# Expert weights split into bf16 pairs ahead of the expert layer instead of inside it, in a four-layer kernel on one core

## The reference

```python
logits = jnp.einsum('btd,de->bte', x, gate_w)
expert_weights, expert_indices = jax.lax.top_k(softmax(logits), 2)
for i in range(8):
    wi = jnp.where(expert_indices == i, expert_weights, 0.0).sum(-1)
    h = silu(x @ w1[i]) * (x @ w3[i])      # 256 -> 1024
    out = out + (h @ w2[i]) * wi[..., None]  # 1024 -> 256
```

## Time and profile before

| what | value |
|---|---|
| median of 3 runs | 864.96 us (863.54 to 866.54) |
| profiled execution | 865.73 us, its span in the trace 864.0 us |
| PE busy | 679.8 us, 79% of the span |
| PE weight loads | 471.9 us, 55% |
| DVE busy | 527.0 us, 61% |
| ACT busy | 410.6 us, 48% |
| POOL busy | 278.8 us, 32% |
| mean granted clock of TensorE | 0.879 of full |
| DMA | 58.41 MB, mean 68 GB/s |

### The profile page before, as it was taken

One profiled execution on the slowest core, in us unless ns is written; L12 is line 12 of the kernel. 1 busy time (PEld: TensorE's weight loads), 2 busy tenths in 40 slices (PEclk: granted clock), 3 DMA queues, 4 the chain that ended last, 5 costly groups with the idle time before them and its releaser, 6 DMA issues.

```text
span 864.0 us, 19336 instructions
## 1 busy us (share of the span) xinstructions
PE 679.8 (79%) x4571; PEld 471.9 (55%) x4615; DVE 527.0 (61%) x1371; ACT 410.6 (48%) x831; POOL 278.8 (32%) x390
## 2 busy tenths in 40 slices
PE   2999999885853991577417989898989998989992
PEld 2788887663322670466404556565656555655661
DVE  5577789985867452788785464646454555464441
ACT  1466655556874463345225444545353545553430
POOL 3111111111436001644302263535354253553421
PEclk9799999986978795555558999999999999999996
DMA  8100000000000114211270514243331525431213
GB/s 260 32 13 12 16 14 13 0 1 1 0 0 12 44 42 159 87 28 27 97 245 19 169 30 132 67 128 73 105 90 31 170 34 165 124 73 24 34 22 110
DMA packets 45844, 58.41 MB, mean 68 GB/s; under 512 B 13497, under 2 KB 39417, under 8 KB 45273
## 3 DMA queue, kind: packets, MB, share of 16 engines
q1 hardware_dynamic: 38328, 47.79, 16.9%
q0 software_dynamic: 7488, 10.31, 7.2%
HBM read 145.90 MB, written 11.80 MB: 183 GB/s over the span
## 4 chain that ended last, share of the span: by engine, by line
PE 48%; DVE 18%; issue 14%; POOL 7%; DMA 3%; ACT 3%; DVEq 2%; POOLq 1%; ACTq 1%; SPq 0%
PE psum L995 16%; PE psum L1017 7%; PE psum L718 3%; PE psum L1008 3%; POOL region L658 3%; PE psum L702 3%; PE psum L725 3%; PE psum L895 2%; PE psum L738 1%; PE psum L757 1%; PE psum L707 1%; PE psum L840 1%; PE psum L888 1%; DVE region L1358 1%; DMA region<-xrow_dram,next_token 1%
## 5 line engine op out<-in xcount | busy, mean ns | idle before, releaser
L995 PE MATMUL psum<-region 128*128 x897 | 209.6, 382 | 19.8 <-POOL pause_p L660 6.2
L995 PEld LDWEIGHTS psum<-region 128*128 128x128 bf16 x936 | 91.6, 98 | 119.1 <-issue 30.4
L1017 PE MATMUL psum<-region 128*128 x936 | 112.5, 278 | 6.2 <-DVE region L1868 3.7
L1017 PEld LDWEIGHTS psum<-region 128*128 128x128 bf16 x936 | 91.3, 100 | 22.3 <-issue 9.2
L1261 ACT ACTIVATE region<-psum 128x512 f32<-128x512 f32 x78 | 46.5, 596 | 115.0 <-PE psum L995 104.2
L1838 DVE TENSOR_TENSOR region<-psum,region 128x512 f32<-128x512 f32 x78 | 53.9, 690 | 72.9 <-ACT region L1261 62.9
L628 POOL TENSOR_TENSOR pause_p<-minus_half 128x1 f32<-128x1 f32 x37 | 7.1, 193 | 191.4 <-DVE next_token L1854 190.6
L640 POOL DMA_INDIRECT sum_dram<-region,tok_idx x39 | 62.0, 1589 | 6.6 <-issue 6.3
L1282 ACT ACTIVATE pause_a<-one_col 128x1 f32<-128x1 f32 x117 | 23.7, 202 | 84.1 <-issue 70.2
L525 POOL TENSOR_TENSOR region<-region,pair_mask 128x256 f32<-128x256 f32 x32 | 18.9, 612 | 137.8 <-ACT region L1062 137.8
L1868 DVE TENSOR_TENSOR region<-psum,region 128x1024 bf16<-128x1024 f32 x39 | 47.6, 1222 | 20.1 <-ACT region L1269 20.1
(11 more groups left out here) (304 smaller groups left out, 1386.0 us busy)
## 6 DMA issues: line engine op xcount, KB each, us to landing
region<-in_L_ffn_w SPq DMA_DIRECT2D x117, 1024.0 KB
region<-in_ctx SPq DMA_DIRECT2D x48, 128.0 KB, 2.1
region<-neg_max_dram SPq DMA_DIRECT2D x4, 1024.0 KB, 7.6
xrow_dram<-region SPq DMA_DIRECT2D x1, 2080.0 KB, 7.8
x_sb<-in_x SPq DMA_DIRECT2D x4, 512.0 KB, 7.1
sum_dram<-x_sb SPq DMA_DIRECT2D x1, 2048.0 KB, 7.5
region<-in_L_ffn_w_down SPq DMA_DIRECT2D x1, 704.0 KB, 8.1
region<-in_L_ffn_w_gate SPq DMA_DIRECT2D x1, 640.0 KB, 8.6
```

Source lines behind the costliest of these rows:

```text
L995: last = mm(psum[:, 2 * f + n, :], (xT_lo if xl else xT_hi)[:, p, k, :], weights_at(place, wl, n, k * F1 + f * FH, FH), start=(i == 0), st ...
L1017: last = mm(psum[:, 7, 0:D], (hT_lo if hl else hT_hi)[:, f, :], weights_at(place, wl, 2, f * D, D), start=(i == 0), stop=(i == 3 * (F1 // ...
```

## The change

All 24 matrices are split before the router. A matrix is a part `i` of 24: the first 18 are those of experts 2 to 7 (`EARLY_PARTS`), the last six those of experts 0 and 1.

- **Early parts, beside attention 0.** SP loads part `i` as f32 into one of three rings in the free `hT` space, POOL issues a second DMA of the same matrix that casts it to bf16 (the high part), POOL subtracts (the low part, four instructions of 512 columns), and SP stores the pair (1 MB) to `split_dram`. POOL does one part after each `mask_k`, its last four around the FFN's start. DVE and POOL wait for all 18 stores before `hT` is written.
- **Late parts, beside the front of attention 1.** SP loads them, POOL casts (four instructions) and subtracts (four), straight to where experts 0 and 1 are read from. Expert 1's pairs are also stored. SP issues these before its `gates_dram` stores, and ACT takes over the `ctx_c` loads, which SP issued before.
- **The expert layer.** SP loads the pairs of the later experts (three DMAs of 1 MB on a condition that is false for experts 0 and 1 where they are), into the slot, for tile `t` after tile `t - 3`. ACT, DVE and POOL have no weights work left, and PE waits for the loads alone. Slots hold matrix by matrix (high, low), no longer all high parts first.
- DVE's copy of two elements at the end of each batch's statistics (line 1388) is now a `tensor_reduce`. ACT asks for its Silu table ahead of the first tile. `gates_all` and `qT_c` moved within `region2`.

The diff, cut to its core:

```diff
+    EARLY_PARTS = 3 * (E - 2)
+    CHUNK = 512
...
+        early_ring = region2[:, 0:3 * 2 * PART].rearrange("p (r n) -> p r n", r=3)
...
+            def load_part(i):                                  # SP
+                view, width = weight_part(i)
+                if i >= (2 if i < EARLY_PARTS else EARLY_PARTS + 2):
+                    sp.wait_ge(part_split, i - 1)
+                sp.dma_start(whole_part(i)[0].rearrange("p (t f) -> p t f", f=width), view).then_inc(part_loaded[ring_of(i)], 16)
+
+            def store_part(i):
+                sp.wait_ge(part_split, i + 1)
+                e, n = part_of(i)
+                sp.dma_start(split_dram[e, n, :, :], whole_part(i)[1]).then_inc(part_stored[ring_of(i)], 16)
...
-            with sp.Fori(0, B // 2 - 1) as i:
-                for p in range(2):
-
-                    sp.wait_ge(t1_done, 2 * i + p + 1)
-                    sp.dma_start(ctx_sb[:, p, :], ctx_in[2 * i + (p + 2), :, :]).then_inc(ctx_loaded[p], 16)
+            load_part(0)
+            load_part(1)
+            for i in range(EARLY_PARTS + 1):
+                if i + 2 < B:
+
+                    sp.wait_ge(t1_done, i + 1)
+                    sp.dma_start(ctx_sb[:, i % 2, :], ctx_in[i + 2, :, :]).then_inc(ctx_loaded[i % 2], 16)
+                if i >= 1:
+                    store_part(i - 1)
+                    if i + 1 < EARLY_PARTS:
+                        load_part(i + 1)
...
+            load_part(EARLY_PARTS)
+            load_part(EARLY_PARTS + 1)
+            for i in range(EARLY_PARTS, PARTS):
+                if part_of(i)[0] == 1:
+                    store_part(i)
+                if i + 2 < PARTS:
+                    load_part(i + 2)
 
             sp.wait_ge(gates_read, B)
...
+            for t in range(NT + 1):
+                if t < NT:
+                    info = info_of(t)
+                    if t >= 1:
+                        sp.wait_ge(gate_up_loaded, 32 * t)
+                    if t >= 3:
+
+                        sp.wait_ge(gu_done, 2 * t - 4)
+                    load_matrix(0, info, gate_up_loaded)
+                    load_matrix(1, info, gate_up_loaded)
+                if t >= 1:
+                    if t >= 2:
+                        sp.wait_ge(down_loaded, 16 * (t - 1))
+                    if t >= 4:
+
+                        sp.wait_ge(dn_done, t - 2)
+                    load_matrix(2, info_before, down_loaded)
...
+            def cast_part(i):                                  # POOL
+                view, width = weight_part(i)
+                if i >= 3:
+                    pool.wait_ge(part_stored[ring_of(i)], 16 * (uses(i) - 1))
+                nc.gpsimd.dma_start(whole_part(i)[1][:, 0:PART].rearrange("p (t f) -> p t f", f=width), view).then_inc(part_cast[ring_of(i)], 16)
+
+            def split_part(i):
+                whole, pair = whole_part(i)
+                pool.wait_ge(part_loaded[ring_of(i)], 16 * uses(i))
+                chunks = [slice(c, c + CHUNK) for c in range(0, PART, CHUNK)]
+                if i >= EARLY_PARTS:
+                    pool.wait_ge(part_split, i)
+                    for c in chunks:
+                        nc.gpsimd.tensor_copy(pair[:, c], whole[:, c]).then_inc(part_high, 1)
+                for n, c in enumerate(chunks):
...
+                    last = nc.gpsimd.tensor_tensor(pair[:, PART:2 * PART][:, c], whole[:, c], pair[:, c], ALU.subtract)
+                last.then_inc(part_split, 1)
...
+            cast_part(0)
+            cast_part(1)
+            for b in range(1, B):
+                mask_k(b, b % 2)
+                split_part(b - 1)
+                cast_part(b + 1)
 
 
             for n, part in enumerate((slice(0, EARLY), slice(EARLY, B))):
+                if n == 1:
+                    split_part(B - 1)
+                    cast_part(B + 1)
+                    split_part(B)
                 pool.wait_ge(ln2_eps, n + 1)
                 nc.gpsimd.tensor_tensor(rstd[:, part], rstd[:, part], minus_half[:, part], ALU.pow).then_inc(rstd2_ready, 1)
+            split_part(B + 1)
+
+            for r in range(3):
+                pool.wait_ge(part_stored[r], 16 * EARLY_PARTS // 3)
...
+            for i in range(EARLY_PARTS, PARTS):
+                split_part(i)
```

204 lines of the change are left out of this document (83 added, 121 removed).

## The result

The changed kernel takes 869.2 us, the median of its 16 runs, against 866.02 us for the kernel before on the same chip: a ratio of **1.0042, 95% interval 1.0025 to 1.006**. It is slower by 0.4%, where 859 us and a gain were forecast. The profiled execution took 867.83 us (before: 865.73), with a span of 865.7 (864.0).

A forecast was written before the change was run, and what follows sets the result against it. PE was taken to bound the expert layer, with DVE near its limit at attention 0's end. The terms -27.0 + 11 + 1 + 9 = -6 and a further us made 865.7 - 7 = 859 us; own range 850 to 868, overall 842 to 890.

The forecast's parts named there:

- The DMAs: Attention 0: a load, a cast and a store fit in a batch, 9.1 of 9.9 us; +1 us for late parts.
- The collisions: End of attention 0: DVE instructions wait for whole POOL instructions at their shared port; +11 us, bounds 0 and 19.
- the rounding of `w_down`: End of attention 0: two POOL chunks meet DVE's rounding of these weights just after the masks; 2.2 us.
- the 12 scalings: End of attention 0: two POOL chunks meet DVE's scalings at 157.67 us; 2.2 us.
- the 12 norms: End of attention 0: DVE's norms at 191.42 us meet the whole split of part 16; up to 4.9, 3 us taken.
- the last norms and what is around them: End of attention 0: four norms, the maximum and line 1497's first roundings meet part 17; up to 4.9, 3.4 us taken.
- the first rival: DVE gets in between POOL's instructions and the front hides the rest; 846 us, chance 0.12.
- Attention 1: Front of attention 1: POOL's six late parts, 7.6 us each, delay the gates' store; +9 us, bounds 4 and 17.
- The experts: Expert layer: 37 tile periods of 9.25 us without weights work, 25.7 us less, and 1.3 ahead of the first tile.
- The DMA bound: Attention 0: the DMA engines become the bound and POOL waits for casted parts before masks; +30 us, 889 us, chance 0.20.
- POOL's casting DMA being long: Attention 0: POOL's DMA for `w2` parts takes 8 us and more, if time goes by rows; +18, 877 us, chance 0.09.
- The expert layer keeping its waits: Expert layer: loads come late or gathers collide with them, PE waits at each change as before; about 880 us, chance 0.04.

The follow-up runs named there:

- start_order: Changed kernel with the first two part loads ahead of the dense weights and the 35 small loads spread over the batches; ratio 0.998 to the kernel before.
- parts_early_2: Second run of the changed kernel with the first two part loads moved ahead of the 35 small loads; 869.12 us, ratio 1.0029 to the kernel before.
- chunk128: Changed kernel with POOL's casts and subtractions of the weights in chunks of 128 columns instead of 512; ratio 1.0271 to the kernel before.
- parts_early: Changed kernel with the first two part loads moved ahead of the 35 small loads, first run; ratio 1.0083 to the kernel before.

## Why the prediction was wrong

It failed by 8.7 us of span (+1.7 for -7), in the terms of its own sum:

- **The DMAs, "+1 us for parts that come a little late": the step that failed.** I asked whether the DMA engines had room, and when parts would land. I did not ask what stands behind the parts' loads in SP's queue at the start, although the change puts two loads of 1 MB right ahead of the first `ctx` loads. It cost 9.0 us: a wait of 6.5 us and the lower clock behind it. start_order gets them back. The Trainium skill (DMA: Bandwidth & Descriptors, "Queues, rings and completion order") states that on each DMA engine the descriptors of one issuing engine's queue are consumed in order; the 8.2 us of a `ctx` load behind 2 MB agree, though parts_early_2's 6.4 us with no part ahead need another reason.
- **The collisions, "+11 us", bounds 0 to 19: right in mechanism and size**, 12.8 measured. By terms: the rounding of `w_down` +1.2 for 2.2 (the mask gap over it is 12.49 us for 11.26), the 12 scalings +2.0 for 2.2 (12.97 for 10.96), the 12 norms +3.9 for 3, the last norms and what is around them +3.2 for 3.4. Of the long roundings the first grew by 0.85 us, but the mask gap over it stayed at 10.86; the second, with the small instruction behind it, cost 0.9 (1.2 forecast for both). The remaining 1.6 us are a term that the sum lacked: PE's matmuls at the lower clock, after it had waited for the longer norms. So the good total is in part luck, terms too large against one left out. That DVE gets in between (the first rival) is refuted.
- **Attention 1, "+9 us": wrong mechanism, too large.** A late part costs 6.9 us, not 7.6, so POOL is through 54 us after `rstd3` and not 59, just before the front, which itself grew by 3.5 us. I had said that what the front loses stays under POOL's time; it was the other way round. chunk128 shows the forecast mechanism, at 10.3 us a part. The lower bound of 4 doesn't follow from its own terms either: casts of 0.5 us and no collisions make 0.4 to 2.8, and 1.27 us for each of the 48 instructions makes 21 instead of the upper 17.
- **The experts, "37 periods of 9.25 us": mis-sized.** They are 9.36. The gain was 21.5 us for 25.7, and 0.1 for 1.3 ahead of the first tile. I took it from quiet tiles of a loop, whose turn costs 0.4 us more at each fourth tile. Another 1.7 us came in by luck, from the clock of the last `down` block, so that the stage as a whole gained 22.8.
- **The DMA bound, 0.20: not it.** The engines' share is 0.99 in the steady part, and masks still come on time; a cast of 1 MB lands in 10.1 us, beside a load and a store in flight, and holds up no mask, though I had let it decide from some 3.7 us on. POOL did wait for parts twice (7.49 us for part 0, 2.97 for part 16), each time until the f32 load was there, and no mask was late by it. **POOL's casting DMA being long, 0.09: refuted**, 0.76 us and at most 0.98, also for `w2`. **The expert layer keeping its waits, 0.04: refuted.** The prices of these last two were loose: 2 us for each of six batches are 12 of the +18, and the costs alone make about 885 us rather than 880.

A saving of 22.8 us was thus given back three times: 9.0 at the start of attention 0, 12.8 at its end, 3.5 in attention 1. The medians agree in direction: +3.15 us where -7 had been forecast.

## What to carry to other kernels

When a large load is added to a queue that also carries small loads that some engine waits for, list that queue in order of issue around the first use, and count both the bytes and the issuing engine's time ahead of each small load. Where TensorE waits, look at the granted clock behind the wait: here 6.5 us of waiting cost 9.0. A DMA share of 0.99 is no bound by itself, if what waits for the transfers was issued early enough. Work put on GpSimd beside VectorE costs whole instructions at their port: keep its instructions short where VectorE is on the path, and long where GpSimd is. Shorter isn't always better: 256 columns gave a stretch of 37.3 us here, 128 gave 38.6, though with another start.

## What the runs showed that I had not expected

- One kernel's start had two outcomes: PE waited 2.98 us for `ctx` in one execution of parts_early and 8.17 in another, 6 us in the end.
- Less work on POOL made attention 1 slower (58.6 us for 55.9), since it drew the next loads closer to the `ctx` loads.
- PE's loop of four tiles cost about 0.2 us in each tile and 0.4 more at each turn; with 34 tiles written out the 37 full periods are 6 to 7 us shorter.
- The last `down` block ran at either clock, 2.81 or 4.2 to 4.5 us, in nine and nine of the 18 profiled executions.
- The share of the DMA engines that the windows give can exceed 1 (1.22 in a window of start_order), so 0.99 does not say that they are full:

```profile
41.00:49.00 8.00, 8.00 (x87) 6.32 (x86) 5.99 (x14) 5.10 (x7) 5.51 (x6) 1.00 1.22 308
```
